# Graph network on one core: where the last layer's gates are made, and look-ups in three bf16 parts

## What is computed

```python
x = _layernorm(x + L0(x, edge_index, edge_attr_32, ...))   # edge MLP, summed by dst
x = _layernorm(x + L1(x, src, dst, ...))                   # gather x[src]*ci, summed by dst
x = _layernorm(x + L2(x, edge_index, ...))                 # dis[row]*dis[col]*x[col], summed by row = src
x = _layernorm(x + L3(x, edge_index, edge_attr_40, edge_weight, node_type, node_vec, ...))
# inside L3, for every edge:
gate = silu(edge_attr @ W1.T + b1) @ W2.T + b2             # needs edge data and weights only
gate = gate + sum(emb[z[src]] * (emb[z[dst]] @ adaptW.T))
cw   = where(distance < 6, 0.5 * (cos(pi * distance / 6) + 1), 0)
msg  = gate * h[dst] * (cw * mult[dst])                    # then summed by src, divided, normalized
```

## Time and profile before

| | us |
|---|---|
| runs without a profile, 3 | 16698.41 to 16702.15, median 16700.2 |
| profiled execution, first to last instruction | 16721.1 |
| scatters of pass 2, first to last start | 8221.80 to 12206.64 |
| scatters of pass 3, first to last start | 12463.49 to 16455.0 |

### The profile page before, as it was taken

One profiled execution on the slowest core, in us unless ns is written; L12 is line 12 of the kernel. 1 busy time (PEld: TensorE's weight loads), 2 busy tenths in 40 slices (PEclk: granted clock), 3 DMA queues, 4 the chain that ended last, 5 costly groups with the idle time before them and its releaser, 6 DMA issues. The chain is left out here.

```text
span 16721.1 us, 272828 instructions
## 1 busy us (share of the span) xinstructions
PE 12086.6 (72%) x57442; PEld 11023.7 (66%) x57443; DVE 9036.3 (54%) x22074; ACT 3218.9 (19%) x9623; POOL 12152.9 (73%) x12612
## 2 busy tenths in 40 slices
PE   7888878887666666666533488988863339888886
PEld 6777777777444444444433488888863338888886
DVE  4776766776554444444422366666652126666667
ACT  1111111111211111111111111111113333333331
POOL 4777777777777777777677777777737777777773
PEclk9999999999555555555555555555555555555555
DMA  5444444444333333333211122222221112232221
GB/s 131 101 102 101 102 101 102 101 102 90 91 85 83 87 85 83 87 85 84 64 41 41 52 74 72 74 73 73 73 52 47 47 51 81 74 83 78 78 79 51
DMA packets 1447655, 1320.81 MB, mean 79 GB/s; under 512 B 958662, under 2 KB 1304425, under 8 KB 1443052
## 3 DMA queue, kind: packets, MB, share of 16 engines
q0 software_dynamic: 450320, 493.60, 12.7%
q1 hardware_dynamic: 502094, 520.02, 12.7%
q10 hardware_dynamic: 495148, 306.20, 6.4%
HBM read 903.35 MB, written 415.31 MB: 79 GB/s over the span
## 5 line engine op out<-in xcount | busy, mean ns | idle before, releaser
L1487 POOL DMA_INDIRECT order<-l_msg,l_uring x6250 | 6066.5, 971 | 1918.4 <-issue 1843.4
L1630 PE MATMUL ps<-l_win,l_oht 32*128 x12500 | 2729.8, 413 | 1996.1 <-DMA l_win<-htab 833.9
L1630 PEld LDWEIGHTS ps<-l_win,l_oht 32*128 32x128 f32 x12500 | 2684.0, 327 | 2037.5 <-issue 2037.5
L489 POOL DMA_INDIRECT l_rows<-btab,l_sd x3125 | 2978.1, 953 | 1128.5 <-issue 1099.7
L1027 POOL DMA_INDIRECT l_rows<-y,l_sd x3125 | 2958.1, 947 | 971.7 <-issue 924.7
L1616 PE MATMUL ps<-l_ordb,l_ohs 128*128 128x49 f32 x15040 | 3278.8, 414 | 377.3 <-DVE l_ohs L1516 184.8
L1616 PEld LDWEIGHTS ps<-l_ordb,l_ohs 128*128 128x128 f32 x15040 | 3231.1, 332 | 429.5 <-issue 334.2
L1528 DVE TENSOR_TENSOR acc<-acc,ps 128x49 f32 x7520 | 1524.5, 206 | 1319.2 <-issue 702.1
L630 PE MATMUL ps<-l_rhs,l_lhs 64*128 x6250 | 1422.0, 423 | 652.3 <-DVE l_rows L566 458.5
L630 PEld LDWEIGHTS ps<-l_rhs,l_lhs 64*128 64x128 f32 x6250 | 1350.8, 328 | 713.4 <-issue 713.4
L645 PEld LDWEIGHTS ps<-l_ohe,l_hid 128*128 128x128 f32 x6250 | 1343.0, 332 | 34.8 <-issue 34.1
(11 more groups left out here) (248 smaller groups left out, 10693.5 us busy)
## 6 DMA issues: line engine op xcount, KB each, us to landing
l_ordb<-order SPq DMA_DIRECT2D x752, 250.0 KB
order<-l_msg,l_uring POOLq DMA_INDIRECT x6250
order<-l_zero ACTq DMA_DIRECT2D x125, 775.0 KB, 4.6
l_dstb<-ids SPq DMA_DIRECT2D x376, 200.0 KB
l_eat<-in_ea40P SPq DMA_DIRECT2D x125, 600.0 KB
gates<-l_gate ACTq DMA_DIRECT2D x125, 600.0 KB
l_gin<-gates SPq DMA_DIRECT2D x125, 600.0 KB
l_rows<-btab,l_sd POOLq DMA_INDIRECT x3125
```

Of the source, the lines that this page charges most:

```text
L489: pool.indirect_dma_start(rows[:, t, :], None, d["btab"], bass.IndirectOffsetOnAxis(ap=sd[:, t, 0:1], axis=0)).then_inc(gat[c], 16)
L1487: pool.indirect_dma_start(d["order"], bass.IndirectOffsetOnAxis(ap=uring[:, t:t + 1], axis=0), msg[:, t, :], None).then_inc(sc[c], 16)
L1630: done = t.matmul(look[c][:, j, :], oht[:, c * CE + j * P:c * CE + (j + 1) * P], win[:, ds((w % 2) * SET + c * LW, LW)], start=False, stop ...
```

## The change

It does these things.
- Pass 1 no longer makes gates or cutoff weights.
- `scatter_pass` makes gates instead, "jobs" of one group of gates each: in pass 2 two jobs in each of the groups 0 to 38 (78 jobs), in pass 3 two jobs in each of the groups 0 to 7 and one in each of the groups 8 to 38 (47 jobs). A job has 5 items, one a chunk; an item is `hidden`, silu, three `gates` matmuls, a copy and a store of its own (120 KB). There is one PSUM bank for `hidden` (`zps`) and one for `gates` (`gps`) where there were two of each.
- On PE the jobs of g stand behind the look-ups of g+1; on ACT they stand at the end of group g, ahead of `begin(0)` of group g+1. On SP the feature loads of g's jobs stand behind the loads of group g, and each waits until the same slot's `hidden` of the jobs before is done.
- The cutoff weights are made group by group in pass 3, three small ACT instructions (`cut_weights`).
- The node tables `y2` and `htab` hold three bf16 parts of every value (value = high + middle + low). `epilogue1` and `epilogue2` make the parts: two more POOL subtractions and two ACT copies a run of 10 blocks. `epilogue1` first loads `ptab` (12,544 rows of 128 bytes), which the prologue used to write straight into `y2`.
- A window is then 96 partitions of bf16 instead of 32 of fp32, the one-hots are bf16 on 96 partitions, ids are broadcast to 96 partitions, and a look-up is one bf16 matmul over all three parts.
- The sums are cleared by ACT behind group 0 instead of by POOL ahead of it.

The core of the diff:

```diff
+SPLIT = 3
+WK = SPLIT * WN
+GATES2 = (39, 0, 0)
+GATES3 = (8, 31, 78)
...
-        win = s.sb("win", [WN, 2 * SET])
-        oht = s.sb("oht", [WN, GE])
+        win = s.sb("win", [WK, 2 * SET], BF16)
+        oht = s.sb("oht", [WK, GE], BF16)
...
+        zps = ps[0:2 * F, NCH * BANK:NCH * BANK + HE]
+        gps = ps[:, (NCH + 1) * BANK:(NCH + 1) * BANK + CT * F]
...
+            def load_features(g, many):
+                for j in range(many):
+                    for c in range(NCH):
+                        sp.wait_ge(z_ready, item0(g, many) + (j * NCH + c + 1 if many == 2 else NCH + c + 1))
+                        sp.nop(nofuse=True)
+                        sp.dma_start(eat[:, j, c, :], a["ea40P"][:, ds(job(g, many, j) * (NCH * HE) + c * HE, HE)]).then_inc(ea_in[j][c], 16)
+            for begin, end, many in spans:
+                with sp.Fori(begin, end) as g:
+                    load_edges(g)
+                    load_features(g, many)
...
-            pool.memset(agg[:, 0:2 * WIDE], 0.0).then_inc(agg_zero, 1)
...
+            def make_hidden(g, many, i):
+                pe.wait_ge(ea_in[i // NCH][i % NCH], (g + 1) * 16)
+                pe.wait_ge(sil_ready, item0(g, many) + i + 1)
+                t.matmul(zps, w1[:, :], eat[:, i // NCH, i % NCH, :], start=True, stop=True).then_inc(z_ready, 1)
+            def make_gates(g, many, i):
+                pe.wait_ge(sil_ready, item0(g, many) + i + 2)
+                pe.wait_ge(made_copied, item0(g, many) + i + 1)
+                for q in range(EV):
+                    ...
+                done.then_inc(made_ready, 1)
+            def jobs(g, many):
+                make_hidden(g, many, 0)
+                for i in range(many * NCH):
+                    if i + 1 < many * NCH:
+                        make_hidden(g, many, i + 1)
+                    make_gates(g, many, i)
...
-            with pe.Fori(0, READ0) as g:
+            with pe.Fori(0, 1) as g:
                 look_up(g)
+            pe.wait_ge(w_in, 8 * 16)
+            for begin, end, many in spans:
+                with pe.Fori(begin + 1, end + 1) as g:
+                    look_up(g)
+                    jobs(g - 1, many)
...
+            def silu(g, many, i):
+                act.wait_ge(z_ready, item0(g, many) + i + 1 + 2 * NCH)
+                nc.scalar.activation(sil[0:2 * F, i % 2, :], zps, ACT.Silu, bias=b1[:, :]).then_inc(sil_ready, 1)
+            def copy_made(g, many, i):
+                ...
+                nc.scalar.activation(made[:, h, :], gps, ACT.Copy).then_inc(made_copied, 1)
+                act.wait_ge(made_copied, item0(g, many) + i + 2)
+                act.nop(nofuse=True)
+                act.dma_start(d["gates"][:, ds(job(g, many, j) * GT + c * CT, CT), :].rearrange("p t f -> p (t f)"), made[:, h, :]).then_inc(made_out[h], 16)
...
+                if gated and many >= 0:
+                    cut_weights(g + 1)
+                if many > 0:
+                    jobs(g, many)
```

More of the change, by code:

```diff
@@ L893, in pass1 @@
         zero = s.sb("zero", [P, pl.ZT * OW])
[L894 to L906, removed]
         lone = s.sb("lone", [P, F])
@@ L978, in _ @@
                 nc.scalar.activation(acc[0:F, k * (pl.NP // 4):(k + 1) * (pl.NP // 4)], bc(zero[0:F, 0:1], [F, pl.NP // 4]), ACT.Copy).then_inc(acc_zero, 1)
[L979 to L1001, removed]
+            with act.Fori(0, NG) as g:
                 act.wait_ge(hot_ready, (g + 1) * NCH)
@@ L1280, in _ @@
             nc.scalar.activation(root[:, :], deg1[:, :], ACT.Sqrt).then_inc(root_ready, 1)
+            act.wait_ge(pt_in, 16)
+            nc.scalar.activation(parts[:, :, 0, F:YW], pt[:, :, :], ACT.Copy).then_inc(p_high, 1)
             act.wait_ge(eps_set, 1)
-            for c in range(n + 1):
+            for c in range(n + 4):
                 if c < n:
@@ L1369, in scatter_pass, with stores, item0, job @@
     gated = layer == 3
+    EV = (CT + 1) // 2
+    HE = EV * P
+    pairs, singles, job0 = (GATES3 if gated else GATES2)
+    JOBS = pairs + singles
+    assert JOBS < READ0 and 2 * GATES2[0] + GATES2[1] == GATES3[2] and job0 + 2 * pairs + singles == (NG if gated else GATES3[2])
+    EDGE = 32 if gated else 16
+    spans = [(begin, end, many) for begin, end, many in ((0, pairs, 2), (pairs, JOBS, 1)) if end > begin]
+    def stores(h):
+        return pairs * NCH + singles * ((NCH + 1 - h) // 2)
+    def item0(g, many):
+        return g * (2 * NCH) if many == 2 else (g + pairs) * NCH
+    def job(g, many, j):
+        return job0 + many * g + j if many == 2 else job0 + pairs + g
     table = d["htab"] if gated else d["y2"]
@@ L1651, in _, with jobs, group @@
+            def jobs(g, many):
+                silu(g, many, 0)
+                for i in range(many * NCH):
+                    if i + 1 < many * NCH:
+                        silu(g, many, i + 1)
+                    copy_made(g, many, i)
+            if gated:
+                cut_weights(0)
+            def group(g, head, many):
                 _starts, _rounds, _before, last = load_group(act, "act", pl, r, g)
@@ L1681, in _ @@
                 clear_look(NCH - 1)
+                if gated and many >= 0:
+                    cut_weights(g + 1)
+                if many > 0:
+                    jobs(g, many)
+            with act.Fori(0, 1) as g:
+                group(g, True, 2)
+            for k in range(4):
+                nc.scalar.activation(agg[:, k * (WIDE // 2):(k + 1) * (WIDE // 2)], bc(zero[:, 0:1], [P, WIDE // 2]), ACT.Copy).then_inc(agg_zero, 1)
+            for begin, end, many in spans:
+                with act.Fori(max(begin, 1), end) as g:
+                    group(g, False, many)
+            with act.Fori(JOBS, NG - 1) as g:
+                group(g, False, 0)
+            with act.Fori(NG - 1, NG) as g:
+                group(g, False, -1)
+            act.wait_ge(w_in, 8 * 16)
+            for h in range(2):
+                act.wait_ge(made_out[h], stores(h) * 16 + 16)
 def epilogue2(nc, pl, a, d, r, ps):
@@ L1766, in _ @@
             act.wait_ge(eps_set, 1)
-            for c in range(n + 2):
+            for c in range(n + 5):
                 if c < n:
```

291 lines of the change are left out of this document (174 added, 117 removed).

## The result

| | us |
|---|---|
| changed kernel, 4 runs | 17473.3 to 17474.9, median 17474.3 |
| kernel before, in the same job, 4 runs | median 16701.2 |
| ratio | 1.0461, interval 1.0447 to 1.0476 |
| profiled execution of the changed kernel | 17472.9 |

The kernel became 773 us, 4.6%, slower. The forecast of 17,265 us was 209 us too low; the range to 17,520 held the time. Of the 209 us, 21 are the step from the profiled execution to the runs: before, the profiled one was 20.9 us above the median, and I took the same off the forecast, but the changed kernel's is within 2 us of its median. The main case had given itself 17,130 to 17,450 us; the time lies in the part of the range that was added for a rival, the late windows.

A forecast was written before the change was run, and what follows sets the result against it. POOL's issuing was taken as the bound, 31.85 us a group in passes 2 and 3. Terms 314 + 123 + 98 + 24 + 10 + 5 − 5 − 5 = +564 us gave 17,265 us; range 16,880 to 17,520.

The forecast's parts named there:

- The main case: Whole kernel: the forecast as worked out, 17,265 us, with its own range 17,130 to 17,450; chance 0.67.
- the late windows: Groups with jobs: SP's windows land 3 us after the one-hots in each of 78 groups, +234, 17,500 us; chance 0.11.
- What bounds the kernel: Passes 2 and 3: POOL's issuing of 25 scatters, 31.85 us a group; pass 1 likewise bound by POOL's gathers.
- The loop: Passes 2 and 3: jobs close a serial chain of ACT, DVE and PE; +314 us in pass 2, +123 and +98 in pass 3.
- The turn of pass 2: Pass 2, once round the serial chain per group: 39.9 us, 8.05 over POOL's, in 39 groups.
- the term of the items: Jobs within a group: one item a 2.44 us, so 26.65 us for two jobs and 14.45 for one.
- The moved clear: Start of pass 2: POOL no longer clears ahead of the first scatter, -5 us; on ACT behind group 0 it costs nothing.
- the ring of waits: Passes 2 and 3: begins, take, one-hots, last look-ups, jobs, and round again, none beside another; 39.9 us in pass 2.
- The epilogues: Between passes: loading `ptab` and making table parts costs +24 us in `epilogue1`, +10 in `epilogue2`; bounds 10 and 70 for both.
- the start of pass 3: Start of pass 3: a few more loads and table loads on ACT, +5 us.
- The clock: PE in the jobs: its clock rises to 2.4 GHz, items become shorter, +180 with the rest, 16,880 us; chance 0.12.

The follow-up runs named there:

- the same work in another order: Changed kernel with jobs of g interleaved between the begins of g+1 on ACT, edges loaded ahead of features, clear behind the last job: 16895.3 us, ratio 1.0115.

## Why the prediction was right, and where its sizes were off

**What bounds the kernel.** Right: pass 1 kept its length without the gates, and with the gates back there every group is at 31.8 us.

**The loop.** Right, and shown by the same work in another order, which brought 578 us back. Its size was taken too small, by 1.8 us in pass 2 and 1.4 in pass 3. The turn of pass 2 lies just over its own bounds (37.5 to 41.5 us) and its term (+389) over its own (220 to 376), so that the range held the time is in part luck: it reached so far up for the late windows, and they did not come. In the group shown, whose turn on ACT is 8375.90 - 8333.93 = 41.97 us against 39.9, the part from `begin(0)` to the first `hidden` took 12.02 us against 12.47 forecast (-0.4). The misses are in the term of the items: from the first `hidden` to the last 22.35 instead of 21.72 us (+0.6), the last `gates` held by the single bank, 3.38 instead of 2.44 (+0.9), the last copy 1.86 instead of 1.48 behind it (+0.4), and ACT's turn of 1.44 instead of 0.8 us (+0.6). Copy and store at the end took 0.1 less. Together that is the 2.1 us. The pass 1 rows, with two banks and other work between, could not show how a run of jobs ends. In pass 3 the forecast calls its 2.80 us the way to the first `take`; the row is the last one's, 12464.63, and the sum needs the last, so its number stands.

**The moved clear.** This step failed. I wrote that it "stands in a loop that has no jobs yet, and costs nothing". Group 0 has jobs, and the clear stands on ACT between its last store and `begin(0)` of group 1, in the ring of waits:

```profile
8324.57 0.37 ACT L1717 ACTIVATE l_made<-ps 128x240 f32<-128x240 f32 x1 [1.73 <-PE ps L1638]
8325.55 8.48 ACT L1773 ACTIVATE acc<-l_zero 128x2401 f32<-128x2401 f32 x4 [0.60 <-ACT l_made L1717]
8333.93 0.35 ACT L1747 ACTIVATE l_msg<-ps 128x240 f32<-128x240 f32 x1
```

The first turns are 58.5 and 63.1 us, 16.8 and 14.5 over the others; 8.5 of each are the clear. The description of the change says both, that the clear stands behind group 0 and that the groups 0 to 38 have jobs. Most of the rest is a wait that I had not seen at all. At the start of pass 2 the ids of group 1 stand on SP behind the ten feature loads of group 0, and DVE's one-hots wait 7.00 us for them; in pass 3 ACT waits 6.45 us for the gates of group 1 and then loads two tables, and DVE waits for its cutoff weights:

```profile
8291.17 3.74 DVE L1553 TENSOR_TENSOR l_oht<-ps,l_dstb 96x640 bf16<-96x640 f32 x5 [7.00 <-DMA l_dstb<-ids]
...
12941.64 0.32 ACT L1700 ACTIVATE l_under<-l_dist,l_six 128x25 f32<-128x25 f32 x1 [6.45 <-DMA l_gin<-gates]
...
12944.29 0.19 DVE L1542 SCALAR_TENSOR_TENSOR l_cwg<-l_under,l_cut 128x25 f32 x1 [7.14 <-ACT l_cut L1706]
```

The gain at the start of pass 2 was real: with fp32 tables and ACT's clear, epilogue 1 is 84.1 us long against 87.9.

**The epilogues.** `ptab` does what was forecast, and the rest beside it was taken too small: the parts of the table cost 118.4 - 84.1 = 34 us in epilogue 1, against +24. PE's wait for the bias is 19.66 us instead of 8.82, 11 us longer where 12 were forecast (first row before, the others after).

```profile
8146.09 42.28 PE L1268 MATMUL ps<-e_wt,acc 48*128 48x48 f32 x196 [8.82 <-DMA e_b<-in_b]
...
8181.42 30.10 PE L1175 MATMUL ps<-e_wt,acc 48*128 48x48 f32 x140 [19.66 <-DMA e_b<-in_b]
8183.45 6.11 POOL L1182 TENSOR_TENSOR e_pt<-e_pt,e_parts 128x3136 f32<-128x3136 f32 x1 [24.18 <-ACT e_parts L1213]
8186.76 3.31 DVE L1254 TENSOR_TENSOR e_u<-e_u,e_b 128x480 f32<-128x480 f32 x1
...
8214.08 6.52 POOL L1194 TENSOR_TENSOR e_parts<-e_pt,e_parts 128x3136 bf16<-128x3136 f32 x1
8215.35 5.77 DVE L1260 SCALAR_TENSOR_TENSOR x<-e_total,x 128x480 f32<-128x480 f32 x1
```

A DVE operation that takes 0.66 us elsewhere took 5.77 us beside POOL's subtraction of 6.52 us, and 3.31 beside the one of 6.11. Those two I had not seen as one piece each. For epilogue 2 I took +10 for the parts and +5 for the start of pass 3, and it is +26. The run with fp32 look-ups, which has the new start and the old epilogue, takes 263.0 us against 256.9, so the start is 6 and the parts are 20. In six of the ten runs of blocks a DVE operation of 0.66 us takes 1.3 to 1.4 beside POOL's subtractions; that this is the whole of the 20 us was not shown.

**The rivals.** The clock stayed at 0.50 in all jobs. By the rule of the Trainium skill ("TensorE: Matmul & The Clock Gate", section "What's actually happening") activity should have opened the gate; the jobs, with PE at 21.35 of 22 us busy between 9100 and 9122, don't agree with it. SP was late once a pass, in the first turns above, and not in the others: the windows are issued by 8378.6, the look-ups that need them start at 8383.94, and over the whole execution the one-hots wait for ids only the 7.0 us of that first turn.

```profile
8373.29 5.28 SPq L1428 DMA_DIRECT2D l_win<-y  x5
...
8383.94 0.51 PE L1658 MATMUL ps<-l_win,l_oht 96*128 x5 [10.77 <-DVE l_oht L1553]
```

Gathers did not get shorter without the gates' traffic, 951 ns against 947.

## What to carry to other kernels

Work is free in a stage only where the order of every in-order engine lets it run beside the bound: put in one block between two links of a ring of waits it cost 682 us here, and spread between them 104. For such a move add up the ring, including turns of loops, the first and last element of the block and anything rare that stands in it, and compare the sum with the bound's period. A second part of a change can have the opposite sign in the new place: the bf16 look-ups and their tables lost 91 us outside the ring and gained 487 in it.

## What the runs showed of the hardware

- The indirect transfers take slightly different times from one program to another: gathers of pass 1 have a median of 947 ns before, 952 in both runs of the changed kernel and in four others with bf16 tables, 944 with fp32 tables and jobs; scatters of pass 2 take 972, 967 and 969. On one slow chip two of these programs had 955 and 971 instead of 952 and 967. Over thousands of them that is 10 to 25 us, and with it pass 0, which the diff does not touch, got 19 us longer. Why was not settled.
- On two chips the kernel before took 46 and 48% longer, though a transfer took as long as elsewhere to within 4 ns and the tail behind the last scatter 267 us against 264. There, while POOL sends indirect transfers, PE steps in many places only once in 2 to 3 us without waiting for a semaphore that the profile shows. These rows are of the version with gates in pass 1:

```profile
3023.52 0.21 PE L649 MATMUL ps<-l_ohe,l_hid 128*128 128x32 f32 x1 [2.22 <-issue]
3026.36 0.21 PE L649 MATMUL ps<-l_ohe,l_hid 128*128 128x32 f32 x1 [2.63 <-issue]
3029.22 0.21 PE L649 MATMUL ps<-l_ohe,l_hid 128*128 128x32 f32 x1 [2.65 <-issue]
```

  In the trace of before 50 of these take 10.88 us in a row. The cause is open. The ranking was another one there: the interleaved kernel beat the kernel before by 1.3%, which it doesn't elsewhere. The traces show where: on one of the two chips pass 1 took 5,491 us with the gates in it and 4,743 to 4,776 without, so moving them out did pay there.
